# A tile's two factors made on VectorE instead of GpSimd, and the scaling of the second exponentials placed on ScalarE or GpSimd by the planned order

## The reference, cut to what matters

```python
p1 = attn_map(q[:, :, :, 0], k[:, :, :, 0])
p2 = attn_map(q[:, :, :, 1], k[:, :, :, 1])
lam = lam1 - lam2 + LAMBDA_INIT
p = p1 - lam * p2
o = jnp.einsum('bhqk,bkhe->bqhe', p, v)
rms = jax.lax.rsqrt(jnp.mean(o * o, axis=-1, keepdims=True) + EPS)
o = o * rms * subln_w
```

## Time and profile before

| | |
|---|---|
| time, median of 3 runs | 1295.33 us (1293.17 to 1296.08) |
| the profiled execution's own time | 1293.83 us |
| its span, first to last instruction | 1292.0 us |
| mean granted TensorE clock in it | 0.989 of full |

### The profile page before, as it was taken

The page is one execution under the profiler, slowest core; times in us unless marked ns, Lnnn a source line. Parts: engine busy times, 40 slices in busy tenths (PEclk is TensorE's granted clock), DMA queues, the critical chain, the costliest instruction groups (busy, mean ns, idle before and its releaser), DMA issues.

```text
span 1292.0 us, 26833 instructions
## 1 busy us (share of the span) xinstructions
PE 1232.1 (95%) x8350; PEld 1071.9 (83%) x8350; DVE 998.0 (77%) x2488; ACT 1069.4 (83%) x2818; POOL 732.4 (57%) x1038
## 2 busy tenths in 40 slices
PE   8899999999999999999999999999996897998998
PEld 6788888888988888889888888788875785886887
DVE  6888888887788788878788878786888789537545
ACT  5889999998799999978899989897888889845341
POOL 3466566554655665637565555465597556565532
PEclk9999999999999999999999999999997999998999
DMA  3244443434354444332643354334333352510001
GB/s 127 64 69 81 74 79 71 87 58 74 52 110 70 73 68 83 66 65 47 105 81 68 71 81 82 67 50 102 67 81 66 60 91 42 131 36 1 29 18 37
DMA packets 298522, 89.86 MB, mean 70 GB/s; under 512 B 289680, under 2 KB 296080, under 8 KB 297872
## 3 DMA queue, kind: packets, MB, share of 16 engines
q1 hardware_dynamic: 297040, 86.58, 35.7%
q10 hardware_dynamic: 1344, 1.57, 0.3%
HBM read 14.71 MB, written 2.10 MB: 13 GB/s over the span
## 4 chain that ended last, share of the span: by engine, by line
PE 67%; DVE 8%; ACT 8%; POOL 7%; issue 5%; DMA 5%; ACTq 0%; SPq 0%; POOLq 0%; DVEq 0%
PE score_bank L993 8%; PE score_bank L999 7%; PE score_bank L996 7%; PE score_bank L1133 7%; DMA p16T<-p 4%; POOL e_all L1687 3%; ACT e_all L1172 3%; PE turn_bank L1098 3%; PE turn_bank L1020 2%; PE turn_bank L1021 2%; PE turn_bank L1022 2%; PE turn_bank L1079 2%; DVE p L1412 2%; PE sum_bank L1020 2%; PE sum_bank L1021 2%
## 5 line engine op out<-in xcount | busy, mean ns | idle before, releaser
L1687 POOL TENSOR_TENSOR e_all<-e_all 128x512 f32<-128x512 f32 (+3 forms) x320 | 373.6, 1188 | 105.2 <-ACT e_all L1187 104.7
L1172 ACT ACTIVATE e_all<-score_bank,negmx 128x512 f32<-128x512 f32 (+2 forms) x640 | 398.7, 635 | 31.9 <-DMA p16T<-p 17.8
L1401 DVE TENSOR_REDUCE mx<-score_bank 128x1 f32<-128x512 f32 (+1 forms) x384 | 243.4, 639 | 46.1 <-PE score_bank L999 43.7
L993 PE MATMUL score_bank<-k_hi,q_hi 128*128 128x512 f32 (+2 forms) x640 | 253.6, 396 | 20.2 <-ACT e_all L1172 13.3
L1412 DVE SCALAR_TENSOR_TENSOR p<-e_all,gain,p 128x512 f16<-128x512 f32 (+3 forms) x320 | 259.5, 826 | 16.1 <-ACT p L1194 15.1
L996 PE MATMUL score_bank<-k_lo,q_hi 128*128 128x512 f32 (+2 forms) x640 | 232.9, 364 | 0.4 <-DVE k_lo L1456 0.4
L999 PE MATMUL score_bank<-k_hi,q_lo 128*128 128x512 f32 (+2 forms) x640 | 232.8, 364 | 0.0
L1194 ACT ACTIVATE p<-e_all,gain 128x512 f16<-128x512 f32 (+3 forms) x320 | 206.7, 673 | 16.5 <-POOL e_all L1687 15.7
L1187 ACT ACTIVATE e_all<-e_all,ratio 128x512 f32<-128x512 f32 (+3 forms) x320 | 198.0, 668 | 10.2 <-POOL ratio L1675 9.8
L993 PEld LDWEIGHTS score_bank<-k_hi,q_hi 128*128 128x128 f32 x640 | 121.5, 190 | 54.8 <-issue 21.0
L1675 POOL TENSOR_SCALAR ratio<-s,inv,neg_lam 128x1 f32<-128x1 f32 x128 | 54.8, 428 | 149.9 <-DVE inv L1666 145.8
(11 more groups left out here) (389 smaller groups left out, 3049.9 us busy)
## 6 DMA issues: line engine op xcount, KB each, us to landing
p16T<-p SPq DMA_TRANSPOSE x320, 3.0
w_raw<-in_w_qkv_dram SPq DMA_DIRECT2D x3, 1024.0 KB, 6.1
w_raw<-in_w_o_dram SPq DMA_DIRECT2D x4, 512.0 KB, 3.4
w_raw<-in_w_ug_dram SPq DMA_DIRECT2D x4, 512.0 KB, 3.8
bv<-in_hidden_dram SPq DMA_DIRECT2D x8, 256.0 KB, 3.0
out_dram<-e SPq DMA_DIRECT2D x16, 128.0 KB, 1.7
e<-in_w_d_dram SPq DMA_DIRECT2D x1, 1024.0 KB, 6.5
x_in<-in_hidden_dram SPq DMA_DIRECT2D x2, 256.0 KB, 3.7
```

The lines of the kernel that those rows point to most:

```text
L993: pe.matmul(bank[:, 0:w], qh, kh, start=True, stop=False)
L1172: act.activation(e, S[k % NS][:, 0:w], ACT.Exp, bias=negmx[:, d % 2, m, s:s + 1], scale=-1.0 if alone else 1.0, accum_out=ssum[:, d % 4, s ...
L1401: dve.tensor_reduce(mx[:, d % 2, m, s, c:c + 1], S[k % NS][:, 0:w], X, ALU.max)\
L1687: pool.tensor_tensor(a, a, b, ALU.add).then_inc(p_pool, 1)
```

## The change

1. `GAIN` moves from POOL to DVE: `ratio` becomes a `scalar_tensor_tensor`, `gain` a `tensor_scalar`, both on 128x1.
2. The epsilon step of `norm` moves from POOL to DVE as an operation of its own, `VE`, after `SQ`. POOL keeps only the power.
3. `E2` may run on POOL. In the plan, `E2` on ACT gets rank 3 instead of 2, and `MIX` waits only for `GAIN`. If POOL comes to a `MIX` whose chunk ACT hasn't begun to scale, POOL gets the scaling as well, right before the `MIX`, and ACT's entry is dropped. If ACT has begun, `MIX` waits for it.

The lists come out with 122 of the 320 scalings on POOL (62 of 512 columns, 50 of 384, 6 of 256, 4 of 128; 24, 31, 28 and 39 in the four groups) and 198 on ACT.

```diff
-                    add("G", "POOL", "GAIN", o, 0.54, [("DVE", "INV", o)] + ([] if o else [("DVE", "LAM2", None)]), 0)
+                    add("I", "DVE", "GAIN", o, 0.16, [("DVE", "INV", o)] + ([] if o else [("DVE", "LAM2", None)]), 0)
...
-                        add("A", "ACT", "E2", (d, jj), 0.19 + 0.00083 * ww, [("POOL", "GAIN", o)], 2)
-                        add("M", "POOL", "MIX", (d, jj), 0.19 + 0.00212 * ww, [("ACT", "E2", (d, jj))], 2)
+                        add("A", "ACT", "E2", (d, jj), 0.19 + 0.00083 * ww, [("DVE", "GAIN", o)], 3)
+                        add("M", "POOL", "MIX", (d, jj), 0.19 + 0.00212 * ww, [("DVE", "GAIN", o)], 2)
...
-            add("N", "POOL", "OT", what, 0.9, [("ACT", "SQ", what)] + ([("DVE", "OP", what - 4)] if what >= 4 else []), 0)
+            add("N", "DVE", "VE", what, 0.08, [("ACT", "SQ", what)], 0)
+            add("N", "POOL", "OT", what, 0.55, [("DVE", "VE", what)] + ([("DVE", "OP", what - 4)] if what >= 4 else []), 0)
...
     def start(engine):
+        for line in (waiting.get(("ACT", "A"), ()),):
+            while line and line[0][1].what in mixed:
+                line.popleft()
...
+                 and not (op.kind == "MIX" and op.what in scaling and ("ACT", "E2", op.what) not in done)]
...
+        if op.kind == "E2":
+            scaling.add(op.what)
+        if op.kind == "MIX":
+            mixed.add(op.what)
+            if op.what not in scaling:
+                orders[engine].insert(-1, ("E2", op.what))
+                us += 0.32 + 0.00085 * duo_chunks(op.what[0])[op.what[1]][4]
...
+                        dve.tensor_scalar(rms_b[:, c], msq[:, c], eps_v[:, g:g + 1], None, ALU.add).then_inc(rms_step, 1)
...
+                        dve.scalar_tensor_tensor(out=ratio[:, d % 4, s:s + 1], in0=s12[:, d % 4, s, 0:1],
+                                                 scalar=inv[:, d % 4, s, 1:2], in1=neg_lam[:, 0:1],
+                                                 op0=ALU.mult, op1=ALU.mult).then_inc(ratio_ready, 1)
+                        dve.tensor_scalar(gain[:, d % 4, s:s + 1], inv[:, d % 4, s, 0:1], full[:, 0:1], None,
+                                          ALU.mult).then_inc(gain_ready, 1)
...
+                        pool.wait_ge(ratio_ready, o + 1)
+                        pool.tensor_scalar(e, e, ratio[:, d % 4, s:s + 1], 0.0, ALU.mult, ALU.add).then_inc(e2_scaled, 1)
```

More of the change, by code:

```diff
@@ L179, in plan @@
     waiting, ending, now, count = {}, [], [0.0], [0]
+    scaling, mixed = set(), set()
     free_at = {e: 0.0 for e in ("PE", "ACT", "DVE", "POOL", "SP")}
@@ L486, in start @@
     def start(engine):
+        for line in (waiting.get(("ACT", "A"), ()),):
+            while line and line[0][1].what in mixed:
+                line.popleft()
         heads = [line[0] for (e, _), line in waiting.items() if e == engine and line]
-        heads = [(op.rank, n, op) for n, op in heads if all(x in done for x in op.after)]
+        heads = [(op.rank, n, op) for n, op in heads if all(x in done for x in op.after)
+                 and not (op.kind == "MIX" and op.what in scaling and ("ACT", "E2", op.what) not in done)]
         if not heads:
@@ L764, in build @@
                 "r_hi", "r_free", "kv_full", "kv_act", "kv_dve", "v_lo", "neg_ready", "sums_ready", "ratio_step",
[L765 removed]
+                "ratio_ready", "gain_ready", "e2_scaled", "e2_act", "p_pool", "p_hi", "p_lo", "pv_done", "o_ready", "msq_ready",
                 "rms_step", "rms_ready")
@@ L811, in build @@
                             neg_use[o, m] = len(neg_use)
+            scaled_by_act = {x: n for n, x in enumerate([x for k, x in orders["ACT"] if k == "E2"])}
+            scaled_by_pool = {x: n for n, x in enumerate([x for k, x in orders["POOL"] if k == "E2"])}
             WORK = (T[0], T[1], R, O)
@@ L1186, in _ @@
                         act.wait_ge(ratio_ready, o + 1)
-                        act.activation(e, e, ACT.Copy, scale=ratio[:, d % 4, s:s + 1]).then_inc(e2_scaled, 1)
+                        act.activation(e, e, ACT.Copy, scale=ratio[:, d % 4, s:s + 1]).then_inc(e2_act, 1)
                     elif kind == "SPLIT":
@@ L1651, in _ @@
                         finish(TILES - 1)
+                    elif kind == "VE":
+                        o = what
+                        c, g = slice(o % 4, o % 4 + 1), o // (2 * DUOS)
+                        dve.wait_ge(msq_ready, o + 1)
+                        if o % (2 * DUOS) == 0:
+                            dve.wait_ge(eps_ready, g + 1)
+                        if o >= 4:
+                            dve.wait_ge(rms_ready, o - 3)
+                        dve.tensor_scalar(rms_b[:, c], msq[:, c], eps_v[:, g:g + 1], None, ALU.add).then_inc(rms_step, 1)
                     elif kind == "SUMS":
@@ L1666, in _ @@
                         dve.reciprocal(inv[:, d % 4, s, :], s12[:, d % 4, s, :]).then_inc(ratio_step, 1)
+                    elif kind == "GAIN":
+                        o = what
+                        d, s = o // 2, tile_of(o)[0]
+                        dve.wait_ge(ratio_step, o + 1)
+                        if o == 0:
+                            dve.wait_ge(lam_step, 2)
+                            dve.wait_ge(lam_ready, 2)
+                        if d >= 4:
+                            dve.wait_ge(p_lo, CHUNKS * (d - 3))
+                        dve.scalar_tensor_tensor(out=ratio[:, d % 4, s:s + 1], in0=s12[:, d % 4, s, 0:1],
[3 more added lines that the diff above has]
+                                          ALU.mult).then_inc(gain_ready, 1)
             @block.gpsimd
             def _(pool):
-                def factor(o):
-                    d, s = o // 2, tile_of(o)[0]
-                    pool.wait_ge(ratio_step, o + 1)
-                    if o == 0:
-                        pool.wait_ge(lam_ready, 2)
-                    pool.tensor_scalar(ratio[:, d % 4, s:s + 1], s12[:, d % 4, s, 0:1], inv[:, d % 4, s, 1:2],
-                                       neg_lam[:, 0:1], ALU.mult, ALU.mult).then_inc(ratio_ready, 1)
-                    if d >= 4:
-                        pool.wait_ge(p_lo, CHUNKS * (d - 3))
-                    pool.tensor_scalar(gain[:, d % 4, s:s + 1], inv[:, d % 4, s, 0:1], full[:, 0:1], 0.0,
-                                       ALU.mult, ALU.add).then_inc(gain_ready, 1)
                 def mix(d, j):
@@ L1685, in mix @@
                     a, b = e1_of(q, w), e2_of(q, w)
[L1686 removed]
+                    if (d, j) in scaled_by_act:
+                        pool.wait_ge(e2_act, scaled_by_act[d, j] + 1)
+                    else:
+                        pool.wait_ge(e2_scaled, scaled_by_pool[d, j] + 1)
                     pool.tensor_tensor(a, a, b, ALU.add).then_inc(p_pool, 1)
                 def norm(o):
[L1690 to L1695 removed]
+                    c = slice(o % 4, o % 4 + 1)
                     pool.wait_ge(rms_step, o + 1)
@@ L1719, in _ @@
                 for kind, what in orders["POOL"] + tail:
-                    if kind == "GAIN":
-                        factor(what)
+                    if kind == "E2":
+                        d, j = what
+                        o, s, _, _, w, _ = duo_chunks(d)[j]
+                        e = e2_of(CHUNKS * d + j, w)
+                        pool.wait_ge(ratio_ready, o + 1)
+                        pool.tensor_scalar(e, e, ratio[:, d % 4, s:s + 1], 0.0, ALU.mult, ALU.add).then_inc(e2_scaled, 1)
                     elif kind == "MIX":
```

10 lines of the change are left out of this document (1 added, 9 removed).

## The result

The changed kernel takes 1309.72 us (median of 4 runs, 1308.62 to 1310.4), against 1295.7 us for the kernel before on the same chip: a ratio of 1.0107, 95% interval 1.0085 to 1.0129. It is **14 us slower** where 7 us faster was forecast, and outside the range. Where one execution of a kernel was slowed as a whole (one of six of `after_ratio_ts`, 2031.75 us at a granted clock of 0.556), it is left out of the times and ratios, and only DVE's own durations are used of its trace.

A forecast was written before the change was run, and what follows sets the result against it. The prediction took PE, busy 95% of the span, as the bound. Its terms, -8 for ACT's relief, +3 for DVE's load and -2 at the folds, gave -7 us: 1295.3 to 1288.3 us, range 1276 to 1301.

The forecast's parts named there:

- (a): PE's score products waiting for exponentials to free banks: less ACT load takes 8 of 19.0 us off; ends 0 and 19.
- (b): Score banks: DVE's added load and epsilon-step waits delay the maxima, then ACT and PE; +3 us, ends 0 and +10.
- the half clock: PE at half speed after the fold stall; worth 7 us at most if the stall goes.
- (c): PE's stall at the folds, behind `k_lo`, shrinks from 8.0 to 6 us; -2 us, ends -13 and +6.
- the sum that was to gate: At the folds, POOL's sum for duo 55's third chunk, holding up ACT's emptying of the bank; 24.1 us from first fold.
- DVE waits in line: Rival, 13%: the epsilon step on DVE waits for ACT's squares and holds up maxima; slower, 1301 us.
- No change: Rival, 18%: PE's waits come from the order's shape, not ACT's load; 1293 to 1298 us.
- Port contention: Rival, 5%: POOL's scalings are held up as its sums were, costing 30 us more on POOL; 1290 us.
- the straight line: POOL scaling cost extended from the 256-column and one-column rows: 0.68 us for 512 columns, 0.58 for 384.

The follow-up runs named there:

- after_ratio_ts: Changed kernel with `ratio` made by tensor_scalar (one tensor, two pointer scalars) instead of scalar_tensor_tensor: 1309.78 us, ratio 1.0096 to the kernel before.
- scale_planned: Kernel before with only the third part of the change, newly planned; factors and epsilon step stay on POOL: 1292.35 us, ratio 0.9969.
- after_no_factors: Changed kernel's lists without the two factor operations on DVE, the inverses standing in for the factors: 1297.07 us, ratio 0.9991 to the kernel before.
- eps_moved: Changed kernel without its factor part, newly planned: epsilon step on DVE, factors on POOL, scalings by the plan: 1309.04 us, ratio 1.0086 to the kernel before.

## Why the prediction was wrong

**(a) Score banks, relief of ACT, -8: wrong.** I took PE's waits for exponentials as ACT's queue and scaled them with ACT's free share. `scale_planned` has the relief without the load on DVE, and these waits stay (19.0 to 22.2 us; 26.9 in `after_no_factors`). The end that I gave for "the exponentials are in truth released late by DVE", 0, came nearest. ACT had waited 13.4 us for `negmx` before and waits 24.5 in `scale_planned` and 31.1 in `after_no_factors`: an ACT that has less to do there waits for DVE instead. The forecast's sign rested on this step.

**(b) Score banks, load on DVE, +3 with ends 0 and +10: this step failed most.** It measured +15 for the two factors (1.0107 against 0.9991), beyond its upper end. The working priced DVE's load as a share of free time and the epsilon step's waits. It had no place for what an instruction delays when it stands in a fixed list ahead of maxima, nor for holds. And it looked only at waits that PE would have, while of the 13 us between those two kernels' spans 11 are busy time, 7 of them by the half clock, which I had priced at the folds alone. That 128x1 takes 205 ns and not 157 was no such error, since starts are only 122 to 131 ns apart.

**(c) The stall at the folds, -2 (8.0 to 6): the number was right by luck**, it is 5.2. The rows of its working in the new trace:

```profile
982.19 0.48 PE L1123 MATMUL proj_bank<-wkv_hi,had 128*128 128x512 f32 x1
993.22 1.60 POOL L1717 TENSOR_TENSOR e_all<-e_all 128x512 f32<-128x512 f32 x1
997.48 0.68 ACT L1328 ACTIVATE k_hi<-proj_bank,su_s 128x512 fp32r<-128x512 f32 x1
1000.34 0.80 PE L1114 MATMUL proj_bank<-xT_hi,wq_hi 128*128 128x256 f32 x2 [5.24 <-DVE k_lo L1592]
```

From the first fold (966.28) to the end of the sum that was to gate, POOL took 28.5 us, not 24.1, ACT then waited for a maximum of DVE (1.2 us), and it took the bank out 15.3 us after its product, not 10.9. But PE wanted it only at 995.10, 12.9 us after the product, where before it was 4.4 and I had added 3.1: it had stood still for 3.3 us in between. Two errors of 4 to 5 us cancel. Nor was the mean clock there the end of it; in the stretch behind, it fell from 0.97 to 0.91.

**The sizes moved.** ACT 987 forecast, 1011 measured; POOL 677 and 693; a POOL scaling of 512 columns 0.68 us and 0.74; DVE 1058 and 1040, since records overlap and the remainders became shorter (259.5 to 245.3 us).

**The rivals.** "DVE waits in line" had the right sign and the wrong mechanism: the epsilon step waited only 6.0 us for ACT's squares, and `eps_moved` alone isn't cheap for another reason, which stays open. Its time, 1301, was too low. "No change" falls. "Port contention" is real and was not the price. The prediction left open who stretches POOL's sums; the trace of before says it: those of 512 columns that begin under a remainder of DVE (27 of 160) take 1592 ns in the median, the others 1280 and never over 1313. The scalings suffer it too, but few: of 62 of 512 columns, 7 begin so and take 1109 ns, the others 692, so the mean is 736 and not the 0.68 us of the straight line. I didn't ask what the same contention does to an operation that is moved *to* DVE with two inputs in SBUF, and the diff said that `ratio` becomes just that; here it was the smaller part.

**What stays open.** In the lists of before, holds and what follows from them make up some 13 of the 18 us. In the changed kernel they are the smaller part: with none, 13.6 us remain of 15, and that for pieces 52 ns longer (the intervals leave some 4 us either way). The remainders, too, were held less there than before (75 of them for 39 us, 94 for 52), so that DVE stood still no longer in all. DVE's small pieces cost about a third of their time there (13.6 us for some 39) and not 0.14. The lists differ, and the clock takes part. How the delays get into PE's busy time, and what makes the pieces dearer there, was not separated; nor why `eps_moved` is slow.

## What to carry to other kernels

Here the price of work moved to an engine that isn't the bound was what stood behind it in that engine's fixed list, not its share of busy time; two unread operations put at the place measure it in one run. A table of waits doesn't: the longer waits of the changed kernel were there without the work too, and taking the work out of the changed kernel's own lists is what showed it. Before moving an elementwise operation to DVE, look at which of its inputs lie in SBUF and what POOL runs at that time, and try the form with one tensor and numbers per row: it won 13 us in the lists of before and nothing that could be measured in the changed ones. And try the parts of a change apart: here the third part was worth 4 to 5 us, and the first two cost 18.
